# Causal masks of the second attention in 64-row tiles, and a bias product with 128 rows

## What is computed

```python
# second attention: 32 heads of 16 features
scores = jnp.einsum('bqhd,bkhd->bhqk', q, k) * scale
scores = jnp.where(causal[None, None], scores, jnp.finfo(scores.dtype).min)
probs = jax.nn.softmax(scores, axis=-1)
out = jnp.einsum('bhqk,bkhd->bqhd', probs, v).reshape(b, s, d)
return out @ wo
# second feed-forward: base product with a bias, router, 8 experts of rank 16
base_out = jnp.einsum('btd,od->bto', x, base_W) + base_b
logits = jnp.einsum('btd,nd->btn', x, router_W) + router_b
...
lora = jnp.einsum('bter,eor->bto', h * w[..., None], B) * SCALING
return base_out + lora
```

## Time and profile before

| what | us |
|---|---|
| median of three runs | 1960.45 |
| profiled execution, its own time | 1953.37 |
| its span in the profile | 1951.6 |
| TensorE busy | 1875.2 |
| VectorE busy | 1511.6 |
| ScalarE busy | 928.2 |
| GpSimd busy | 908.6 |
| mean granted clock of TensorE | 0.984 of full |

### The profile page before, as it was taken

One profiled execution on the slowest core, in us unless ns is written; L12 is line 12 of the kernel. 1 busy time (PEld: TensorE's weight loads), 2 busy tenths in 40 slices (PEclk: granted clock), 3 DMA queues, 4 the chain that ended last, 5 costly groups with the idle time before them and its releaser, 6 DMA issues.

```text
span 1951.6 us, 37656 instructions
## 1 busy us (share of the span) xinstructions
PE 1875.2 (96%) x12504; PEld 1539.5 (79%) x12504; DVE 1511.6 (77%) x2386; ACT 928.2 (48%) x2297; POOL 908.6 (47%) x872
## 2 busy tenths in 40 slices
PE   8999978999999999999999999998999999998997
PEld 3688867888888888888888888886798856666776
DVE  2577747878888888888888888888789668889886
ACT  1333324444444444444444444454655378888333
POOL 0133344444444444444444444363486668887111
PEclk9999988999999999999999999998999999999999
DMA  9577741111111111111111111321387786553111
GB/s 345 177 238 246 231 153 41 49 49 49 49 49 48 48 47 41 45 43 48 48 48 48 48 48 46 95 80 62 104 239 229 232 239 181 156 158 105 43 60 60
DMA packets 201703, 211.12 MB, mean 108 GB/s; under 512 B 19066, under 2 KB 172666, under 8 KB 200604
## 3 DMA queue, kind: packets, MB, share of 16 engines
q1 hardware_dynamic: 200692, 209.27, 34.7%
q10 hardware_dynamic: 936, 0.85, 0.1%
HBM read 128.14 MB, written 73.53 MB: 103 GB/s over the span
## 4 chain that ended last, share of the span: by engine, by line
PE 71%; issue 11%; DVE 9%; POOL 4%; SPq 2%; DMA 1%; ACT 1%; POOLq 0%; DVEq 0%; ACTq 0%
PE ps L1063 18%; PE ps L1024 16%; PE ps L1037 7%; PE ps L1052 5%; PE ps L1075 4%; DVE f_neg_max L2033 4%; PE ps L1047 3%; PE ps L1849 3%; PE ps L2652 2%; POOL k_rot L571 2%; PE ps L2616 2%; PE ps L2152 2%; PE ps L2210 2%; SPq L1348 2%; PE ps L2158 1%
## 5 line engine op out<-in xcount | busy, mean ns | idle before, releaser
L1063 PE MATMUL ps<-wo,ot 128*128 (+1 forms) x1536 | 388.5, 402 | 0.0
L1063 PEld LDWEIGHTS ps<-wo,ot 128*128 128x128 f32 x1536 | 282.7, 190 | 58.7
L818 ACT ACTIVATE prob<-ps,neg_max 128x128 f32<-128x128 f32 (+1 forms) x512 | 208.6, 421 | 132.7 <-DVE neg_max L899 109.7
L1024 PE MATMUL ps<-ht_hi,wq 128*128 (+1 forms) x1024 | 255.4, 392 | 5.9 <-DVE q_swap L892 5.9
L978 POOL TENSOR_TENSOR q_rot<-q_rot,q_swap 128x512 f32<-128x512 f32 x128 | 164.8, 1288 | 180.0 <-DVE q_swap L892 175.4
L825 ACT ACTIVATE pt<-ps 128x512 fp32r<-128x512 f32 x192 | 108.1, 597 | 283.6 <-PE ps L1075 283.5
L1024 PEld LDWEIGHTS ps<-ht_hi,wq 128*128 128x128 f32 x1024 | 193.1, 189 | 48.0 <-issue 6.3
L972 POOL TENSOR_TENSOR prob<-prob,inv_sum 128x512 f32<-128x512 f32 x64 | 66.7, 1042 | 293.3 <-DVE inv_sum L908 293.3
L571 POOL TENSOR_TENSOR k_rot<-k_rot,k_swap 128x512 f32<-128x512 f32 x32 | 60.2, 1884 | 190.7 <-DVE k_swap L476 190.7
L1037 PE MATMUL ps<-pt,vv 128*128 128x512 f32 x576 | 144.5, 395 | 3.4 <-issue 2.9
L874 DVE TENSOR_TENSOR ot<-ps,ot 128x512 fp32r<-128x512 f32 x128 | 88.3, 691 | 76.4 <-ACT ot L835 76.3
(11 more groups left out here) (248 smaller groups left out, 4125.7 us busy)
## 6 DMA issues: line engine op xcount, KB each, us to landing
stack_dram<-e_part SPq DMA_DIRECT2D x192, 128.0 KB, 2.4
v_dram<-v_part SPq DMA_DIRECT2D x32, 512.0 KB, 5.9
k_dram<-k_part SPq DMA_DIRECT2D x64, 256.0 KB, 2.5
kk<-k_dram SPq DMA_DIRECT2D x128, 128.0 KB, 2.1
vv<-v_dram SPq DMA_DIRECT2D x128, 128.0 KB, 2.1
f_q<-stack_dram SPq DMA_DIRECT2D x124, 104.0 KB
f_k<-stack_dram SPq DMA_DIRECT2D x124, 104.0 KB
wmod<-in_wmod SPq DMA_DIRECT2D x12, 1024.0 KB, 12.2
```

Of the source, the lines that this page charges most:

```text
L818: nc.scalar.activation(p[:, h], sc[:, h], ACT.Exp, bias=neg_max[:, t, h:h + 1], accum_out=row_sum[:, t, h:h + 1]).then_inc(p_exp, 1)
L1024: mm = nc.tensor.matmul(ps_q[j][:], w[:, at:at + HD0], r[:, bass.ds(b, 2), k], start=(n == 0), stop=(n == len(passes) - 1))
L1063: mm = nc.tensor.matmul(ps_y[j][:], o[:, j, h * P:(h + 1) * P], w[:, bass.ds(at + h * D, D)], start=(n == 0), stop=(n == len(passes) - 1))
```

## The change

A new table `halves` of four blocks of 128 columns is loaded: the two 64-row halves of the identity and the two of the mask, each stacked twice, so that both the lower and the upper 64 partitions hold them. Each mask product becomes two of 64 rows (`part` 0 and 1), in the same tile as the scores of its e. In the loop the early masks stand behind the far shifted scores and no longer start a group. In `begin`, ahead of the loop, only the tiles change. The bias product gets 128 rows: bias zero and row one in the added ones. A helper `put_masks` outside the stage, which nothing called, is deleted.

```diff
+    halves = sb("halves", [P, 4, P])
...
             sp.dma_start(wmod[n % NW][:], io["wmod"][l][:, :, v * D:(v + 1) * D]).then_inc(wmod_in[n % NW], 16)
+        sp.dma_start(halves[:], io["halves"]).then_inc(halves_in, 16)
         sp.wait_ge(mod_done, len(mods) // GROUP)
...
-        nc.vector.tensor_copy(keep.ident_b[:], keep.ident[:])
-        nc.vector.tensor_copy(keep.mask_b[:], keep.mask[:])
+        dve.wait_ge(halves_in, 16)
+        nc.vector.tensor_copy(keep.halves_b[:], halves[:])
...
-    def put_mask(t, e):
-
-        mask = keep.mask_b[:].rearrange("p (o k) -> p o k", o=1).broadcast_to([P, 2, P])
-        nc.tensor.matmul((s0, s1)[t][:, e, :, t * P:(t + 1) * P], keep.ident_b[:], mask,
-                         start=True, stop=False, skip_group_check=True)
+    def put_masks(t, first):
+
+        for part in range(2):
+            for e in range(2):
+                rows = slice(64 * e, 64 * e + 64)
+                mask = keep.halves_b[rows, 2 + part].rearrange("p (o k) -> p o k", o=1).broadcast_to([64, 2, P])
+                nc.tensor.matmul((s0, s1)[t][:, e, :, t * P:(t + 1) * P], keep.halves_b[rows, part], mask,
+                                 start=first and not part, stop=False, skip_group_check=True)
...
-        for e in range(2):
-            put_mask(1, e)
+        put_masks(1, True)
...
-                if at < U - 2:
-                    mask_early()
                 shifted_near(v, slot)
                 shifted_far(v, slot)
+                if at < U - 2:
+                    put_masks(0, False)
...
-    bias_raw = first.tile("g_bias_raw", [33, D])
-    bias = first.tile("g_bias", [33, D], F32R)
-    row = last.tile("g_row", [33, P])
-    row_r = last.tile("g_row_r", [33, P], F32R)
+    bias_raw = first.tile("g_bias_raw", [P, D])
+    bias = first.tile("g_bias", [P, D], F32R)
+    row = last.tile("g_row", [P, P])
+    row_r = last.tile("g_row_r", [P, P], F32R)
...
-        keep.ident_b, keep.mask_b = sb("ident_b", [P, P], BF16), sb("mask_b", [P, P], BF16)
+        keep.halves_b = sb("halves_b", [P, 4, P], BF16)
...
+        "halves": np.stack([np.tile(t[i:i + 64], (2, 1)) for t in (np.eye(P, dtype=np.float32), mask) for i in (0, 64)], 1),
```

More of the change, by code:

```diff
@@ L116, in setup0 @@
     table_in = sem("table_in")
+    halves_in = sem("halves_in")
     copied = sem("copied")
@@ L2170, in scores_late @@
             score(pe, slot, 1, e, 1).then_inc(s_done, 1)
-    def mask_early():
-        for e in range(2):
-            put_mask(0, e)
     def scores_early(pe, u, slot):
@@ L2195, in begin @@
             pe.wait_ge(keep.p_mul, 4 * B + 1)
-            mask_early()
+            put_masks(0, True)
             scores_early(pe, 0, 0)
```

## The result

The changed kernel takes 1943.6 us, the median of five runs (1941.7 to 1947.99); the kernel before has 1959.25 in the five runs beside them. The ratio is 0.9933, with a 95% interval of 0.9913 to 0.9953: 13 us faster, between 9 and 17. (The two medians alone are 15.7 apart; that lies inside the interval.) A second set of six runs gives 0.9933 again (0.9918 to 0.9948). The forecast was 13.5 us and 1947.0, the latter against the 1960.45 of the first three runs.

What follows compares the result with a forecast made beforehand. TensorE, busy 96% of the span, with VectorE in the second attention's chain and TensorE alone in the output stage. 7.8 + 5.7 = 13.5 off the median of 1960.45 gives 1947.0; own range 1941 to 1952, whole range 1940.5 to 1955.5.

Steps and rivals of the forecast that it cites:

- The path: Second attention: masks are on the path twice; late masks in 64-row tiles bring the period from 3.53 to 3.37.
- early masks' move "along the path": Second attention: early masks behind the far shifted scores change nothing, zero; bounds 0.05 better and 0.22 worse.
- The load waits: Second attention: a load behind the table loads is awaited about 1 us; shorter periods ahead give back 0.5.
- before the first start I count no gain: Second attention, before its first regular start: the stage waits for transfers, so no gain is counted there.
- Masks, total: Second attention: 0.16 x 52 = 8.3 us, less 0.5 for the load wait, leaves 7.8.
- Bias product: Output stage: 128 rows save 0.38 sixteen times, 6.1; the last element gives 0.4 back, leaving 5.7.
- The last element's wait for g_mid: Output stage, last element: TensorE can come only 0.34 earlier, not 0.76, because of VectorE's g_mid; 0.4 given back.
- A: Second attention, rival: the mask pairs don't overlap, each mask group takes 0.44; 1957.9, half of it 1951; chance 0.10.
- the rule named beside it: Trainium skill: weights overlap matmuls only across differing row groups; second mask pair and scores would wait, 1957.9.
- B: Second attention, rival: VectorE is the limit already, so the attention gains nothing; 1954.7; chance 0.08.
- C: Second attention, rival: masks pay a changeover at each product, four take 1.12, not 0.22; 2030; chance 0.04.
- D: Output stage, rival: the bias product keeps its stalls, which come from its wait or operands, not rows; 1952.7; chance 0.06.

Runs made afterwards that it cites:

- bias half: The kernel before with only the bias product given 128 rows, masks as before: ratio 0.9968 to the kernel before.
- the halves: Two kernels against the kernel before: new masks only, bias product kept at 33 rows, ratio 0.9974; bias product only, masks as before, ratio 0.9968.

## Why the prediction held, and where not

**The path.** Right. Masks stood on it twice; the late ones held the second reduction, and only as much as VectorE's own pace let go. For the forecast period of 3.37, 3.34 was measured; late masks alone in tiles gave 3.37.

**The early masks' move "along the path" at no cost.** Taken as zero against the kernel before, and 0.03 a unit better: the early scores end 1.44 behind the turn for the forecast's 1.42, but the reduction starts 0.02 behind them, not 0.07. Two things of opposite sign make up the 0.03: the tiles alone, at the old place, take the period from 3.37 to 3.28, and the move costs 0.06 of that. The prediction had one price for a changeover; the rows have two, 0.10 into masks and 0.20 into scores. The bound of 0.05 on the better side was there; that the old place would give more than it was not seen.

**The load waits.** Undersized: 0.5 us was put down for the wait behind the tables. The sum of stretches rose from 2.6 (mean of three profiles with old masks) to 6.3 (mean of three with the new ones at the change's period), by 3.7. Of this some 1.6 lies in units 4 and 5, at the lower clock, and some 2.1 behind the loads of weights and tables, for which 0.5 was the term. The step "before the first start I count no gain" was too kind as well: that part came 0.8 later in the mean. The units ahead of the stores' arrival run quicker into it, TensorE idles for 4.63 in place of 0.89, and unit 4 runs at 1.2 GHz. What the idle time does to the clock is in no term of the sum.

**Masks, total.** Forecast 7.8, measured 5.1 (3.3 to 6.8); the period won more than forecast (9.9 for 8.3), the stretches took 3.7 of it, and what is left lies within the scatter.

**Bias product.** Right: forecast 0.23 and 2.78, measured 0.23 and 2.77; forecast 5.7, measured 6.3 (4.1 to 8.2), 6.5 by the two profiles (157.0 and 150.5 from the last turn to the end). The last element's wait for g_mid came, 0.52 in the weight loads. That the two profiles give 6.5 all the same is chance: a piece at the lower clock ahead of it was shorter after (six expert products 2.42 for 2.93). Its length varies in both kinds of kernel. With 33 rows the last whole element takes 18.33 and 18.44 in two profiles and 17.30 to 17.58 in three; with 128 rows 17.31 to 17.57 in five and 16.78 to 16.81 in four. Between the three and the four the stage is 5.7 shorter (156.1 to 156.3 against 150.5), which is the forecast.

**Rivals.** A fell: pairs run side by side. So did the rule named beside it: the four weight loads of a mask group, the second pair's on the rows of the first, are all done 0.12 us after the first starts, while its products run for 0.40. B fell: the 0.16 came. C fell: four masks in a row take 0.23. D fell in the bias half alone. By the halves the gain is 5.1 + 6.3 = 11.4, by the whole 13; both lie within the intervals. The total of 13.5 is closer to 13 than the attention's term was to its own value, and that is luck: the masks came 2.7 short by the halves, the bias product 0.6 over.

**What stays open.** Why the sum of stretches varies between 0.8 and 4.4 in the same program. The runs' scatter of 6 us is not that alone: the first mask product starts anywhere from 1554.6 to 1560.8 us in the fourteen profiles, which is scatter of the stages ahead (1556.9 to 1560.8 without the new table, 1554.6 to 1560.1 with it, so its load and cast cost nothing that shows). With the early masks gone or back at the old place, the runs' difference to the change (0.9912 and 0.9931 against 0.9933) is smaller than the periods say; the sums of stretches in their profiles (9.9 and 6.7) account for part, for no masks in the loop; for the old place they don't differ enough.

## What to carry to other kernels

Small matmuls that switch between full and half rows pay at each switch, in the product behind it too, so count pieces of the chain and not durations of instructions; zero rows that keep the mode cost nothing (a bias product of 128 rows takes 0.23, like each product behind it). When a stage gets quicker ahead of a transfer that lands at a fixed time, look at what TensorE's idle time does to its clock behind it: here unit 4 alone took 2 us longer. Before moving an operation along a path, ask whether it is needed: the early masks only sharpened a maximum, and without them, with big loads cut into pieces, the kernel came to 0.987. That is a change of arithmetic, though: where a masked score lies far above those that are kept, all exponentials of its row can come out as zero. No run here tries such inputs.

## What was not expected of the hardware

- A changeover between 128 and 64 rows costs 0.10 us ahead of the mask products, with two-byte weights (0.32 or 0.33 for 0.22 or 0.23), and 0.20 ahead of the shifted scores, with four-byte ones (0.61 for 0.41), at the full clock.
- Behind a load of 1 MB in the same queue a load of 104 KB landed after 6.10 us, and after 6.37 at a DMA share of 0.97; with the megabyte in four pieces and a unit's loads between, no such wait is left.
- After 4.63 us without a matmul the granted clock was 0.50 for the next unit, which then took 5.50 in place of 3.34; after 0.89 us it was 1.00, and after 1.53 us, in the second profile of the kernel before, 0.65 from 1585 to 1588.
